# A 12-stage decoder kernel: one early load of the rotary weights in the latent attention's preamble, and a new place for two products of the second mixer in three sequences

## The reference, cut to what matters

```python
proj = hidden_states @ in_proj_w.T
gate, hBC, dt = jnp.split(proj, [INTER, INTER + CONV_DIM], axis=-1)
# causal convolution of four taps, bias, silu over hBC; xs, B, C = split(hBC)
dt = jnp.clip(jax.nn.softplus(dt + dt_bias), DT_MIN, DT_MAX)
# decays L = exp(segment sums of -exp(A_log) * dt), G = C B^T
# y = (G * L) @ (xs * dt) + D * xs;  y = y * silu(gate), rms norm, @ out_proj_w.T
```

```python
kv_c = kv @ W_kvc
q_c = q @ W_dq
q_nope = (q_c @ W_uq).reshape(b, lq, H, HD).transpose(0, 2, 1, 3)
q_rope = (q_c @ W_qr).reshape(b, lq, H, R).transpose(0, 2, 1, 3)
...
x1, x2 = (x[..., :half], x[..., half:])
return jnp.concatenate([x1 * cos - x2 * sin, x1 * sin + x2 * cos], axis=-1)
```

## Time and profile before

| what | value |
|---|---|
| median of 3 runs | 2342.03 us (2338.34 to 2343.21) |
| profiled execution, its own time | 2342.29 us |
| its span (first to last instruction) | 2340.5 us |
| TensorE busy | 2079.5 us (89%) |
| VectorE busy | 1609.6 us (69%) |
| ScalarE busy | 1238.2 us (53%) |
| GpSimd busy | 304.3 us (13%) |
| mean granted TensorE clock | 0.941 |
| second mixer, main loop | from about 960 us to 1200 us of the span |
| latent attention, first block | from about 1201 us to 1220 us |

### The profile page before, as it was taken

How to read it: one execution, slowest core, us unless ns; L and a number is a source line. 1 busy time by engine, 2 the same in 40 slices (tenths; PEclk the granted TensorE clock), 3 DMA queues, 4 the chain that set the end, 5 groups by cost and what they waited for, 6 DMA issues and landing times. The chain is left out here.

```text
span 2340.5 us, 46706 instructions
## 1 busy us (share of the span) xinstructions
PE 2079.5 (89%) x18816; PEld 1584.9 (68%) x18816; DVE 1609.6 (69%) x2987; ACT 1238.2 (53%) x2455; POOL 304.3 (13%) x309
## 2 busy tenths in 40 slices
PE   7978989899899898888879898979899878999996
PEld 4644458677555687566657666758566658999996
DVE  5756656677565897877858877867566676667663
ACT  2325664454466454555546457554478615666663
POOL 0010000111310000001000000000100114434432
PEclk9988999899999998999989999989889979999998
DMA  3020010100100002000020000010200025666663
GB/s 119 22 65 24 12 43 1 37 1 1 59 20 5 31 1 71 1 1 1 1 78 10 9 9 0 0 37 1 73 1 2 6 97 193 198 209 210 199 212 88
DMA packets 62648, 125.57 MB, mean 54 GB/s; under 512 B 16056, under 2 KB 45369, under 8 KB 62297
## 3 DMA queue, kind: packets, MB, share of 16 engines
q1 hardware_dynamic: 53626, 110.83, 14.1%
q0 software_dynamic: 8832, 12.06, 2.5%
HBM read 109.18 MB, written 15.80 MB: 53 GB/s over the span
## 5 line engine op out<-in xcount | busy, mean ns | idle before, releaser
L262 PE MATMUL ps<-ffn_xh,ffn_wh 128*128 128x256 f32 x644 | 184.1, 286 | 1.5 <-DVE ffn_xl L4334 1.5
L262 PE MATMUL ps<-ffn_xh,ffn_wl 128*128 128x256 f32 x644 | 182.5, 283 | 0.0
L262 PE MATMUL ps<-ffn_xl,ffn_wh 128*128 128x256 f32 x644 | 182.3, 283 | 0.0
L4329 DVE TENSOR_TENSOR ffn_wl<-ffn_fresh,ffn_wh 128x1792 fp32r<-128x1792 f32 x69 | 139.4, 2023 | 27.0 <-ACT ffn_wh L4209 27.0
L210 POOL TENSOR_TENSOR all_rstd<-all_mv,all_cst 128x4 f32<-128x4 f32 x41 | 9.4, 229 | 1020.4 <-DVE all_mv L193 1020.3
L1962 DVE SCALAR_TENSOR_TENSOR attn_xc<-attn_cx,all_w,attn_xc 128x512 f32<-128x512 f32 (+1 forms) x144 | 107.2, 749 | 50.3 <-ACT attn_xc L1813 46.9
L4209 ACT ACTIVATE ffn_wh<-ffn_fresh 128x1792 fp32r<-128x1792 f32 x69 | 117.0, 1695 | 15.1 <-DMA ffn_fresh<-in_l3f_w 15.1
L262 PEld LDWEIGHTS ps<-ffn_xh,ffn_wh 128*128 128x128 f32 x644 | 123.6, 192 | 1.7 <-DVE ffn_xl L4334 1.7
L262 PEld LDWEIGHTS ps<-ffn_xl,ffn_wh 128*128 128x128 f32 x644 | 123.5, 192 | 0.0
L262 PEld LDWEIGHTS ps<-ffn_xh,ffn_wl 128*128 128x128 f32 x644 | 123.4, 192 | 0.0
L2988 ACT ACTIVATE xattn_sc<-xattn_sc,xattn_mx 128x128 f32<-128x128 f32 x256 | 98.8, 391 | 17.7 <-DVE xattn_mx L3085 17.7
(11 more groups left out here) (483 smaller groups left out, 6111.0 us busy)
## 6 DMA issues: line engine op xcount, KB each, us to landing
ffn_fresh<-in_l3f_w SPq DMA_DIRECT2D x69, 896.0 KB, 4.9
all_w<-in_ctxT SPq DMA_DIRECT2D x12, 512.0 KB, 5.7
all_w<-in_ctx SPq DMA_DIRECT2D x8, 512.0 KB, 6.8
all_x<-in_x_rows SPq DMA_DIRECT2D x4, 512.0 KB, 7.4
all_x<-x_seq SPq DMA_DIRECT2D x4, 512.0 KB, 5.3
all_w<-in_l2x_o SPq DMA_DIRECT2D x1, 2048.0 KB, 9.2
all_w<-in_l2f_up SPq DMA_DIRECT2D x1, 2048.0 KB, 8.7
xattn_ctxT<-in_ctxT SPq DMA_DIRECT2D x4, 512.0 KB, 3.7
```

The source lines that it names most:

```text
L262: last = pe.matmul(out, a, b, start=start and n == 0, stop=stop and n == 2)
L4329: dve.tensor_tensor(wl[:, j % 2, piece(q)], fresh[:, piece(q)], wh[:, j % 2, piece(q)].bitcast(F32), ALU.subtract).then_inc(low_ready.sem, 1)
```

## The change

In the mixer, `early(q)` is true for the larger mixer where t = 0 and a next group exists: q = 0, 4 and 8. There VectorE issues `weigh` of the first two tiles of sequence q + 1 right after `values(q + 1)`, ahead of `step_bias`, `conv` 0 and `conv` 1, and leaves them out at the start of the next loop. No instruction is added or dropped.

In the latent attention's first block SP issues the whole W_qr once, the segment ids and the context ahead of `after`; the two loads by halves are gone. `raw` holds W_qr once. ScalarE rounds it whole, and then writes the exchanged form by two instructions of half the size that read and write pieces of 32 columns; VectorE's second remainder is split likewise. The waits on `small` are for 32 (two loads) in place of 64.

```diff
@@ mixer, block.vector
+            def early(q):
+                return PADDED and q % TG == 0 and q // TG < last_group
+
             for q in range(BATCH):
                 g, t = q // TG + 1, q % TG
                 more = g <= last_group
+                first_weighed = q >= 1 and early(q - 1)
                 for i in range(PT):
-                    weigh(PT * q + i)
+                    if not (first_weighed and i < PU):
+                        weigh(PT * q + i)
                     if q >= 1 and i == PU - 1:
                         add(q - 1)
...
                 gated(q)
                 if q + 1 < BATCH:
                     values(q + 1)
+                if early(q):
+                    for i in range(PU):
+                        weigh(PT * (q + 1) + i)
                 if more and t == 0:
                     step_bias(g)
@@ phase_xattn2
-        raw = qL[0:MQ, 0:4, :].rearrange("p a t -> p (a t)").rearrange("p (s h r) -> p s h r", s=2, h=MH)
+        raw = qL[0:MQ, 0:2, :].rearrange("p a t -> p (a t)").rearrange("p (h r) -> p h r", h=MH)
+        def by_head(a, s):
+            return a[:, s].rearrange("p a b -> p (a b)").rearrange("p (h r) -> p h r", h=MH)
@@ block.sync
-                after(sp)
-                qr = k.ins["l2x_qr"].rearrange("c (h r) -> c h r", h=MH)
-                sp.dma_start(raw[:, 0], qr).then_inc(small.sem, 16)
-                sp.dma_start(raw[:, 1, :, 0:half], qr[:, :, half:MR]).then_inc(small.sem, 16)
-                sp.dma_start(raw[:, 1, :, half:MR], qr[:, :, 0:half]).then_inc(small.sem, 16)
+                sp.dma_start(raw[:, :, :], k.ins["l2x_qr"].rearrange("c (h r) -> c h r", h=MH)).then_inc(small.sem, 16)
                 sp.dma_start(seg_i[:, :], k.ins["seg"]).then_inc(small.sem, 16)
                 sp.dma_start(ctxT[:, :, :], sources_xattn1(k)[1][0]).then_inc(ctx_loaded.sem, 16)
-                sp.wait_ge(*small(0, 64))
+                after(sp)
+                sp.wait_ge(*small(0, 32))
@@ block.scalar
-                act.wait_ge(*small(0, 64))
-                for s in range(2):
-                    act.activation(wh[:, ROPE + s].rearrange("p a b -> p (a b)"),
-                                   raw[:, s].rearrange("p h r -> p (h r)"), ACT.Copy).then_inc(rounded.sem, 1)
+                act.wait_ge(*small(0, 32))
+                act.activation(by_head(wh, ROPE), raw[:, :, :], ACT.Copy).then_inc(rounded.sem, 1)
+                act.activation(by_head(wh, SWAP)[:, :, 0:half], raw[:, :, half:MR], ACT.Copy).then_inc(rounded.sem, 1)
+                act.activation(by_head(wh, SWAP)[:, :, half:MR], raw[:, :, 0:half], ACT.Copy).then_inc(rounded.sem, 1)
@@ block.vector
-                dve.wait_ge(*small(0, 64))
+                dve.wait_ge(*small(0, 32))
                 dve.tensor_copy(seg_f[:, :, 0], seg_i[:, :])
-                for s in range(2):
-                    dve.wait_ge(*rounded(0, s + 1))
-                    dve.tensor_tensor(wl[:, ROPE + s].rearrange("p a b -> p (a b)"), raw[:, s].rearrange("p h r -> p (h r)"),
-                                      wh[:, ROPE + s].rearrange("p a b -> p (a b)").bitcast(F32), ALU.subtract)
+                dve.wait_ge(*rounded(0, 1))
+                dve.tensor_tensor(by_head(wl, ROPE), raw[:, :, :], by_head(wh, ROPE).bitcast(F32), ALU.subtract)
+                dve.wait_ge(*rounded(0, 3))
+                for a, b in ((slice(0, half), slice(half, MR)), (slice(half, MR), slice(0, half))):
+                    dve.tensor_tensor(by_head(wl, SWAP)[:, :, a], raw[:, :, b], by_head(wh, SWAP)[:, :, a].bitcast(F32), ALU.subtract)
```

## The result

The changed kernel takes 2328.55 us (median of 5 runs, 2323.28 to 2331.01) against 2341.91 us (5 runs): the ratio is 0.9941, with a 95% interval of 0.9925 to 0.9958, so 13.8 us less, between 9.8 and 17.6 (the two medians differ by 13.4). The forecast was 2333.0, 9.2 us less, in a range from 2329.0 to 2338.0. The direction was right, and the gain was larger than the range allowed. Later kernels were measured beside new runs of before, whose medians were 2340.87, 2339.75 and 2340.92 us; what they gain or lose is told by the ratio.

The account below looks back on a forecast made before the run. VectorE was taken to set the pace in the mixer run and a late ids load to delay the latent block; 6.8 + 2.4 = 9.2 us less gave 2333.0 us, range 2329.0 to 2338.0.

Parts of the forecast that it names:

- the sum: Whole kernel: mixer 6.8 us plus latent block 2.4 us gives 9.2 us less, to 2333.0 us.
- The mixer's edit, 6.8 us: Sequences 1, 5 and 9: two `weigh` move from VectorE's busy run into idle time, 2.27 us gained in each.
- given back: Rival, mixer: each 2.27 us becomes a longer wait for ScalarE's `pad`; only 2.4 us left, 2339.9; chance 0.10.
- priced that at 1.3 us: Rival "slower", work after 972 us: low-clock stretches in more places cost 1.3 us each, 2347 with 11 to 12; chance 0.04.
- the tightest: Sequence 9, mixer: decay 38 done at 1115.94, VectorE ready for it at 1116.05; hidden by 0.1 us.
- The latent block's edit, 2.4 us: Latent attention's first block: ScalarE's 2.46 us wait for the ids goes; block's work ends at 1217.0, not 1219.41.
- where the forecast had 3.5: Latent block: its last remainder comes some 3.5 us after ScalarE's last copy, not 5.9.
- forecast 1.25: Latent block: VectorE's second remainder, split into two halves, takes 1.25 us; bounds 1.18 and 2.4.
- the forecast's 3.5: Next stage's weights, queued behind 904 KB more, land up to 3.5 us later, still ahead of ScalarE's copy.
- The rival on the clock: Shorter gaps keep TensorE at 2.4 GHz: 1.8 us less at the latent block's products, 0.6 in the mixer; 2330.5; chance 0.14.

Follow-up runs that it names:

- idle products: Changed kernel plus TensorE products of no use in the gap at the end of the latent block's first block: eight 2326.00 us, four 2322.11 us.
- the order alone: Changed kernel, but all three W_qr loads, ids and context go ahead of the next stage's weights and rounding stays in two whole instructions: 2325.09 us.
- a pause of 1.2 us: Changed kernel plus one VectorE addition that nobody reads, at the start of layer 2's feed-forward stage: 2331.48 us, ratio to before 0.9966.
- 2.3 us more: Kernel before plus two VectorE additions that nobody reads, at the start of layer 2's feed-forward stage: 2339.32 us, ratio 1.0003.

## Why the prediction was right or wrong

The step that failed is the sum: 6.8 + 2.4 = 9.2 us takes each edit's gain to the end of the kernel and puts what TensorE's clock does behind them at nothing. In its place the runs showed 4.2 to 5.4 us less in untouched work, some 1.2 us of the latent block's gain given back at once, and 8.7 us for the mixer in the mean of the profiles, all three, as far as the profiles show, by low-clock stretches that moved.

**The mixer's edit, 6.8 us: right in its mechanism, and a little short.** The decays were in time, `step_bias` was 0.8 us late at no cost, the third `weigh` starts 4.88 us after `conv` (4.87 by the forecast's sum), and the shift goes on through outputs, rows and features; the rival "given back" is ruled out. In the nine profiles with the edit the three groups take 191.8 to 196.1 us, in the five without it 201.5 to 202.6: between 5.4 and 10.8 us less, 8.7 in the mean. What the sum lacked is again the clock. In the second group the stretch with `pad` ran at 0.75 before, and the prediction priced that at 1.3 us, but only as something that could get worse. In the changed kernel it ran at full clock:

```profile
1037.00:1042.00 5.00, 5.00 (x29) 4.21 (x30) 3.37 (x5) 2.60 (x5) 0.24 (x1) 1.00 0.00 0
```

From the end of `values` to the first `conv` sequence 4 took 1043.23 - 1036.66 = 6.57 us before and takes 1041.18 - 1035.89 = 5.29 now: those 1.3 us, besides the 2.27. In the third group it can be seen both ways. First the changed kernel (VectorE's rows of sequences 8 and 9, and the clock of the stretch):

```profile
1101.60 2.38 DVE L1992 TENSOR_TENSOR attn_e<-attn_e,all_w 128x1024 f32<-128x1024 f32 x2 [1.18 <-ACT attn_e L1846]
...
1107.47 2.33 DVE L1962 SCALAR_TENSOR_TENSOR attn_xc<-attn_cx,all_w,attn_xc 128x512 f32<-128x512 f32 x3 [3.28 <-ACT attn_xc L1813]
...
1113.36 2.36 DVE L1992 TENSOR_TENSOR attn_e<-attn_e,all_w 128x1024 f32<-128x1024 f32 x2 [0.61 <-ACT attn_e L1846]
...
1104.00:1109.00 5.00, 5.00 (x13) 3.85 (x12) 1.68 (x3) 1.36 (x3) 0.00 (x0) 0.50 0.00 0
```

Then its second profile:

```profile
1101.52 4.56 DVE L1962 SCALAR_TENSOR_TENSOR attn_xc<-attn_cx,all_w,attn_xc 128x512 f32<-128x512 f32 x6 [1.53 <-ACT attn_xc L1813]
...
1106.40 2.35 DVE L1992 TENSOR_TENSOR attn_e<-attn_e,all_w 128x1024 f32<-128x1024 f32 x2
...
1098.00:1103.00 5.00, 5.00 (x27) 4.13 (x27) 3.44 (x5) 2.58 (x5) 0.00 (x0) 1.00 0.00 0
```

At a clock of 0.50 VectorE waits 3.28 us for the first `pad` and 0.61 us for decay 38, the point that the forecast called the tightest; at full clock 1.53 us and nothing. The forecast had 0.1 us to spare at that decay. The first profile of the changed kernel shows the smaller gain, by some 3.5 us in this group.

**The latent block's edit, 2.4 us: right for the block, wrong for what follows it.** ScalarE's last copy ends at 1208.54 and the last remainder at 1211.93: 3.39 us, where the forecast had 3.5 and before 5.91. The split halves take 1.28 us (forecast 1.25), SyncE is not last. The next stage's weights are issued at 1197.75 and land 13.5 us later, 1211.3, or 15.4 us after the block's first product (1195.87) and not 12.5 (1213.3 against 1200.80): 2.9 us later than before, within the forecast's 3.5, and 1.2 us ahead of ScalarE's copy. The Trainium skill says in "DMA: Bandwidth & Descriptors", section "Queues, rings and completion order", that each DMA engine takes the descriptors of a queue in ring order. The trace agrees with its 2.9 us. In the kernel with all loads early ScalarE does wait for these weights, 4.12 us, some 2 us more than for the end of the block.

What failed is the term's way into the sum, 2.4 us kept to the end. The second block's first eight products run at the low clock for longer than before, 3.78 + 2.99 us against 3.62 + 1.88, and some 1.2 us of the 2.5 go at once. The profiles without idle products all say the same: behind a gap of 4.4 to 4.5 us these eight take 6.5 to 6.8 us, behind 5.6 us 6.2, and behind 6.5 to 7.0 us 5.9 to 5.3. So about half of what the gap loses comes back as low clock. The rival on the clock had the right place with the wrong sign: it gave the shorter gap a chance of a gain of 1.8 us and none of a loss. The Trainium skill, in "TensorE: Matmul & The Clock Gate", section "HAM oscillation", says that gaps of TensorE can send it back to 1.2 GHz. The trace agrees: the clock was 0.50 behind the 4.46 us that were left, and 1.00 behind a gap of 0.83 us.

**The sum.** It lacked a term: 4.2 to 5.4 us less for the 417 us of work between 1543 and 1960. The prediction saw the mechanism, but only as a cost with a chance of 0.04 ("if low stretches fell in more places, 1.3 us each") or as 1.8 and 0.6 us at two named places. It didn't ask for the low stretches that stood in before's own trace behind both edits, and so didn't see that there was something to gain as well. With the terms as means of the profiles of before and of these edits it is 8.7 (mixer) + 1.2 (latent block, 28.4 to 27.2) + 4.6 (behind it, 416.2 to 411.6) = 14.5 us, within the measured 9.8 to 17.6. The range reached to 2329.0 for the clock's rival and scatter; it should have held the stretches that are in reach of a shift.

## What to carry to other kernels

Cost a reordering by the timeline of the engine that sets the pace: what moves from its busy run into its idle time is gained in full where the others wait for it, and that held to 0.1 us here in the local rows. Then look at the granted clock behind the edit, and widen the range, on both sides, by the low stretches that stand there: a shift of a few us moves them, at 1.5 us each. Where TensorE has a gap of some us ahead of a burst that others wait for, a few products of no use that end just before the burst can be worth more than the gap's shortening (2.9 against 1.3 us here); too many delay it.

## What the runs showed of the hardware that I had not expected

That the low-clock stretches are not noise. Four executions (the changed kernel twice, the latent edit alone, the order alone) took 411.5 to 411.7 us for the work from 1543 to 1960, though they reached it at 1529 to 1544 us of their spans; and a pause of 1.2 us made the same work 4.5 us longer. Nothing here shows why executions that differ in their first 958 us by up to 4.5 us come to the same placing; that stays open.

That 1.2 us more of work can cost 5 to 6, and 2.3 us more nothing that can be measured. A comparison of two kernels by 10 us is, on such a program, in part one of placings, whatever was edited.
